# One buffer for the turned probabilities, and the value products ahead of the next unit's first turn

## The reference

```python
def _L1_xattn_ref(query, key, value, W_Query, W_Key, W_Value, W_Output, B_Query, B_Key, B_Value, B_Output):
    H, D = (16, 64)                       # heads, width of one
    q = query @ W_Query + B_Query         # 8 x 512 x 1024
    k = key @ W_Key + B_Key
    v = value @ W_Value + B_Value
    ...                                   # each split into heads
    scores = jnp.einsum('bqhd,bkhd->bhqk', q, k) / D ** 0.5
    probs = jax.nn.softmax(scores, axis=-1)
    out = jnp.einsum('bhqk,bkhd->bqhd', probs, v)
    out = out.reshape(B, Lq, H * D)
    return out @ W_Output + B_Output
```

## Time and profile before

| what | value |
|---|---|
| median of 3 runs | 1952.4 us (1950.66 to 1956.3) |
| the profiled execution | 1943.8 us, span 1942.0 us |
| PE busy | 1713.6 us, 88% of the span |
| DVE busy | 1208.7 us, 62% |
| ACT busy | 842.5 us, 43% |
| POOL busy | 642.4 us, 33% |
| mean granted clock of TensorE | 0.925 of full speed |

### The profile page before, as it was taken

One profiled execution on the slowest core, in us unless ns is written; L12 is line 12 of the kernel. 1 busy time (PEld: TensorE's weight loads), 2 busy tenths in 40 slices (PEclk: granted clock), 3 DMA queues, 4 the chain that ended last, 5 costly groups with the idle time before them and its releaser, 6 DMA issues. The chain is left out here.

```text
span 1942.0 us, 26422 instructions
## 1 busy us (share of the span) xinstructions
PE 1713.6 (88%) x8927; PEld 1166.4 (60%) x8927; DVE 1208.7 (62%) x2741; ACT 842.5 (43%) x1870; POOL 642.4 (33%) x761
## 2 busy tenths in 40 slices
PE   6389999995999999999999999999999996721674
PEld 4267777673666666666666666666666664721453
DVE  5535444424777777777777777777777775567351
ACT  3333434423555555555555555555555552100221
POOL 2244454431233232333323223223323322102685
PEclk9779999998999999999999999999999998555877
DMA  7100000004312212222222222222222220501443
GB/s 247 20 22 12 12 12 1 1 0 122 66 44 66 66 44 65 66 46 64 66 48 62 66 49 60 66 51 59 66 50 60 66 54 26 165 1 44 88 81 51
DMA packets 66656, 109.45 MB, mean 56 GB/s; under 512 B 16088, under 2 KB 48096, under 8 KB 66528
## 3 DMA queue, kind: packets, MB, share of 16 engines
q1 hardware_dynamic: 60384, 99.29, 20.7%
q0 software_dynamic: 6144, 8.52, 2.8%
HBM read 27.84 MB, written 12.85 MB: 21 GB/s over the span
## 5 line engine op out<-in xcount | busy, mean ns | idle before, releaser
L1018 POOL TENSOR_SCALAR at_Pr<-at_Pr,at_rinv 128x512 f32<-128x512 f32 x512 | 354.1, 692 | 827.5 <-DVE at_rinv L1045 827.5
L997 ACT ACTIVATE at_Pr<-at_ps,at_nmax 128x512 f32<-128x512 f32 x512 | 352.0, 687 | 524.3 <-DVE at_nmax L1040 522.7
L1040 DVE TENSOR_REDUCE at_nmax<-at_ps 128x1 f32<-128x512 f32 x512 | 350.8, 685 | 139.9 <-PE at_ps L905 129.0
L905 PE MATMUL at_ps<-at_k,at_q 128*128 128x512 f32 x1024 | 420.6, 492 | 10.1 <-DMA at_k<-at_k_own 8.4
L916 PE MATMUL at_ps<-k_ident,at_Pr 128*128 128x128 f32 x2048 | 311.1, 275 | 4.0 <-POOL at_Pr L1018 4.0
L916 PEld LDWEIGHTS at_ps<-k_ident,at_Pr 128*128 128x128 f32 x2048 | 249.7, 140 | 93.4 <-POOL at_Pr L1018 32.9
L1052 DVE COPY at_PT<-at_ps 128x512 f32<-128x512 f32 x384 | 261.3, 681 | 0.0
L905 PEld LDWEIGHTS at_ps<-at_k,at_q 128*128 128x128 f32 x1024 | 174.6, 191 | 129.4 <-issue 120.0
L926 PE MATMUL at_ps<-at_PT,at_V 128*64 128x512 f32 x1024 | 235.9, 603 | 0.9 <-DVE at_PT L1052 0.9
L1045 DVE RECIPROCAL at_rinv<-at_rsum 128x1 f32<-128x1 f32 x512 | 83.3, 163 | 174.4 <-ACT at_Pr L997 172.4
L926 PEld LDWEIGHTS at_ps<-at_PT,at_V 128*64 128x64 f32 x1024 | 68.2, 138 | 123.1 <-issue 122.0
(11 more groups left out here) (251 smaller groups left out, 2102.3 us busy)
## 6 DMA issues: line engine op xcount, KB each, us to landing
at_k<-at_k_own SPq DMA_DIRECT2D x256, 256.0 KB, 4.1
k_x<-in_x SPq DMA_DIRECT2D x8, 512.0 KB, 7.7
mg_ctx<-in_ctx SPq DMA_DIRECT2D x8, 512.0 KB, 7.8
mx_ctxn<-in_ctx SPq DMA_DIRECT2D x8, 512.0 KB, 3.9
rows<-lo_xn SPq DMA_DIRECT2D x8, 512.0 KB, 3.0
out<-k_x SPq DMA_DIRECT2D x1, 4096.0 KB, 14.6
ex_w_in<-in_L_ffn_w SPq DMA_DIRECT2D x16, 256.0 KB, 2.9
mx_w<-in_L_ffn_w SPq DMA_DIRECT2D x2, 1024.0 KB, 10.4
```

Source lines behind the costliest of these rows:

```text
L905: ins = pe.matmul(ps[:, S_BANK + j % 2, :], q2[:, u % 2, h, q:q + P], k2[:, u % 2, h, part, :], start=part == 0, stop=part == 1)
L997: act.activation(Pr[:, j % 4, :], ps[:, S_BANK + j % 2, :], ACT.Exp, bias=nmax[:, j % 4:j % 4 + 1], accum_out=rsum[:, j % 4:j % 4 + 1]).th ...
L1018: pool.tensor_scalar(Pr[:, n % 4, :], Pr[:, n % 4, :], rinv[:, n % 4:n % 4 + 1], 1.0, ALU.mult, ALU.mult).then_inc(s["pn"], 1)
L1040: dve.tensor_reduce(nmax[:, j % 4:j % 4 + 1], ps[:, S_BANK + j % 2, :], AX.X, ALU.max, negate=True).then_inc(s["nmax"], 1)
```

## The change

`PT` loses its index `u % 2` and keeps half its size. On PE, `weigh_values(u - 1)` goes ahead of turn 0 of `u`. On DVE, each `keep` waits for `pv` to reach `u` as well, which `weigh_values(u - 1)` raises.

```diff
-        PT = sb("PT", [P, 2, 2, TPB, S], F32)
+        PT = sb("PT", [P, 2, TPB, S], F32)
 ...
-                                            PT[:, u % 2, h, t, :], start=t == 0, stop=t == TPB - 1)
+                                            PT[:, h, t, :], start=t == 0, stop=t == TPB - 1)
 ...
                         if there(u):
                             score(u, j)
+                        if j == 2 and there(u - 1):
+                            weigh_values(u - 1)
+                        if there(u):
                             if j >= 2:
                                 turn(u, j - 2)
                         if j < 2 and there(u - 1):
                             turn(u - 1, NBL - 2 + j)
                         if j < 2 and there(u + 1):
                             project(u + 1, j)
-                        if j == 2 and there(u - 1):
-                            weigh_values(u - 1)
 ...
-                            act.copy(PT[:, u % 2, (j - 2) // TPB, :, q:q + P],
+                            act.copy(PT[:, (j - 2) // TPB, :, q:q + P],
 ...
                     dve.wait_ge(s["t_ps"], NBL * u + j + 1)
+                    wait_count(dve, s["pv"], u)
                     q = P * (j % TPB)
-                    dve.tensor_copy(PT[:, u % 2, j // TPB, :, q:q + P],
+                    dve.tensor_copy(PT[:, j // TPB, :, q:q + P],
```

## The result

The changed kernel takes 2026.41 us (median of 4 runs, 2022.77 to 2027.65) against 1952.88 us (4 runs). The ratio is 1.0372, 95% interval 1.0351 to 1.0393: slower by 73.5 us. The forecast was 2018 us, range 1998 to 2038, and slower.

What follows compares the result with a forecast made beforehand. PE's own order of work was taken to bound the attention. 62 units at 1.05 us plus 0.4 us for unit 63 gave 65.5 us, added to the 1952.4 us median: 2018 us, range 1998 to 2038.

Steps and rivals of the forecast that it cites:

- The place and the mechanism: DVE's late copy 0 holds the keys and reciprocal 2, so PE's turn 2 waits 1.13 us; unit 1.05 us later.
- The chain from copy to turn 2: DVE's copy 0 through reciprocal 2 and POOL's scaling to PE's turn 2: 2.32 us, read from unit 0.
- Score 2 to products to turn 0: PE's new order: 0.87 + 0.10 us to the products, then 3.59 us to turn 0, its weight load not pulled ahead.
- Turn to copy: From turn 0's start on PE to copy 0's start on DVE: 0.64 us, at most 0.81.
- The value products and copy 7: PE's products need DVE's copy of block 7: margin 0.4 us, where it was 0.97; nothing booked.
- The added wait: DVE's copies also wait for pv, which never ends last: booked at 0, with 0.17 us kept for the range.
- The cover of the keys' DMAs: SP's DMAs of the keys land 4.1 us after issue, leaving 3.4 us before the next unit's score 0.
- Turn 6's wait: PE's turn 6 waits for POOL's block, about 0.45 us a unit; expected to stay as it is.
- A free order: Rival: PE keeps its work, so moving turn 0 costs nothing, 1952 us; chance 0.04.
- a gain by the change-overs: Rival: PE's switches between full-width and half-width matmuls vanish, up to 0.25 us a unit, 1937 us; chance 0.02.
- a smaller delay: Rival: a shorter wait at turn 6 gives back at most 0.45 of 1.05 us a unit, 1970 to 1998; chance 0.09.
- The clock: Rival: two waits a unit lower TensorE's granted clock, 113 us more, 2131; chance 0.05, shared with products waiting for copy 7.

Runs made afterwards that it cites:

- Experiments 3: Changed kernel with the next unit's keys and reciprocal 2 moved ahead of copy 0 on DVE: ratio 0.9988 to the kernel before, unit 18.12 us.
- 4: Changed kernel with only the next unit's keys moved ahead of copy 0 on DVE: ratio 1.0154 to the kernel before, unit 18.67 us.
- 1: Kernel before with the single buffer and the added wait for pv, PE's old order kept: ratio 1.0357, unit 19.25 us.
- experiments 2: Kernel before with the new PE order alone, two buffers and no added wait: ratio 1.0373, unit 19.32 us.
- 5: Kernel before with a wait for pv added to each DVE copy, at a value long reached (u - 1): ratio 0.9989, unit 18.16 us.
- sixth kernel: Changed kernel with the next unit's value projection ahead of turn 2 on PE: ratio 1.0168 to the kernel before, unit 18.64 us.
- eighth kernels: Changed kernel with the next unit's value projection ahead of turn 2 and query projection ahead of turn 6 on PE: ratio 1.0170 to the kernel before.
- seventh kernel: Kernel before with the next unit's query projection ahead of turn 6 on PE: ratio 0.9949, unit 17.97 us.

## Why the prediction was right, and where its sizes were off

- **The place and the mechanism** were right: copy 0 late by the products, the keys and reciprocal 2 queued behind it, turn 2 waiting for POOL, nothing given back after score 5. Experiments 3 and 4 show it by taking away what was queued, 1 by making the copy late in another way.
- **The chain from copy to turn 2** was taken from unit 0 at 2.32 us; it is 2.33 (1005.72 to 1008.05).
- **Score 2 to products to turn 0** was to take 0.97 and 3.59 us; it is 0.96 and 3.59. The weight load of turn 0 behind the products shows the same 0.81 us put down to issue as score 3's did, in 63 units. So the row was the right guide. The Trainium skill ("TensorE: Matmul & The Clock Gate", What happens when you issue a matmul) says that TensorE's queue can pull a weight load ahead of running matmuls; this trace shows no such pull at this place. Whether the change from half-width to full-width matmuls is the reason was not tested.
- **Turn to copy** was sized too low: 0.64 us by turns whose weight loads run ahead, 0.70 for turn 0 behind the products, whose four transposes take 0.66 instead of 0.60. The same stretching lengthens the step from the late turn 2 to the value projection from 0.43 to 0.49. These two terms of 0.06 us bring the forecast's 1.05 us a unit to the measured 1.16, and its 65 us to 72. This is the sum's main miss.
- **The value products and copy 7.** The margin was put at 0.4 us (the prediction's own 0.97 us from score 2 to products makes it 0.5) and nothing was booked. In the steady unit copy 7 ends at 1000.83 and the products start at 1001.43 without a wait. In unit 63, where PE has no projections of a next unit, they did wait for it, 0.65 us, and score 2 to products is 1.38 us. There turn 2 also comes 1.05 us after score 4, where it was 0.55, and 0.3 us of that is given back before score 5. So unit 63 with the tail cost 0.8 us in place of 0.4.
- **The added wait** was booked at 0 with 0.17 as a bound; experiments 2 and 5 give 0.
- **The cover of the keys' DMAs** was wrong, though it did not decide. The prediction added one DMA's 4.1 us to the end of the keys, and left out that four are issued one after the other. In the changed kernel they start at 1007.14 and their issue takes 3.14 us; with the 6.9 us that the sixth kernel shows from the first issue to score 0, `k2` is there near 1014.0, and score 0 comes at 1014.70. The cover is 0.7 us by this estimate, not 3.4, and behind the start of the attention two scores did wait for the DMAs, 0.5 us in all. The sixth and eighth kernels used it up.
- **Turn 6's wait** was called about 0.45 us a unit and expected to stay. It stayed (score 5 to turn 6 is 5.13 us, 1010.25 to 1015.38, and was 5.14), but it was worth 0.19 us, as the seventh kernel shows.
- **The rivals.** A free order, a gain by the change-overs, and a smaller delay are excluded by the unit of 19.32 us. The third kernel, where the new order costs nothing, is 0.04 us a unit under the kernel before: that is the net worth of the new order on PE, change-overs and the stretched turn together, not 0.25. The clock stayed at 1.00 in the steady units.

## What to carry to other kernels

In an in-order queue, ask of every instruction whose input you delay what stands behind it and who waits for that; moving two short instructions of the next chain ahead of the copy made a 3.7% loss vanish, and left the buffer saved. Read the price of a wait from the distance of starts, not from the idle time of a weight load. And count every issue of a group of transfers when you work out its cover, not the landing of one.

## What the runs showed of the hardware that was not expected

- A wait of 0.41 us on a weight load delayed the matmuls by only some 0.18 us; the two matmuls of score 0 (1008.36, 0.71 us) ran during most of it.
- Four transposes whose weight loads had no matmul to hide under took 0.66 us and released DVE after 0.69 to 0.70 us; with hidden loads they take 0.60.
- Four 256 KB DMAs on SP's queue took 3.1 us to issue and 6.9 us from the first issue to the score that waited for them.
- One wait of 1.0 us in each unit of 19.3 us left the granted clock at 1.00. In unit 63, where PE waited 0.32, 1.10 and 0.65 us in short order, it fell to a mean of 0.72 between 1696 and 1702 us, that is, to the lower level of 1.2 GHz for a part of them; the kernel before, with waits of 0.32 and 1.10 us, shows the same mean between 1612 and 1618 us.
